# Queries turned unsplit two sequences ahead and stacked from DRAM, on a gated cross-attention block

## The reference

```python
q = relu(layernorm(x)); k = v = relu(ctx)            # per head of 32
att = softmax(q k^T / sqrt(32)); o = att v
x1 = x + tanh(g0) * relu(o @ ffn_w.T + ffn_b)
n = layernorm(x1); n_prev = n shifted by one token
xr = mu_r*n + (1-mu_r)*n_prev; xk likewise with mu_k
out = x1 + tanh(g1) * sigmoid(xr W_r) * (relu(xk W_k)^2 W_v)
```

## Time and profile before

| what | value |
|---|---|
| median of 3 runs | 2935.4 us (2933.75 to 2940.07) |
| the profiled execution | 2935.97 us |
| its span | 2934.1 us |
| mean granted clock of PE | 0.996 |
| busy share PEld, DVE, ACT, POOL | 74%, 80%, 53%, 36% |
| DMA | 408.56 MB, mean 139 GB/s |

### The profile page before, as it was taken

How to read it: one execution, slowest core, us unless ns; L and a number is a source line. 1 busy time by engine, 2 the same in 40 slices (tenths; PEclk the granted TensorE clock), 3 DMA queues, 4 the chain that set the end, 5 groups by cost and what they waited for, 6 DMA issues and landing times. The chain is left out here.

```text
span 2934.1 us, 71298 instructions
## 1 busy us (share of the span) xinstructions
PE 2833.1 (97%) x23168; PEld 2183.8 (74%) x23168; DVE 2349.9 (80%) x4175; ACT 1568.1 (53%) x2828; POOL 1044.8 (36%) x902
## 2 busy tenths in 40 slices
PE   3899999999999999999999999999999999999998
PEld 2677777777777777777777777777777777777776
DVE  5788888888888878878878878888888888888874
ACT  4455555555555555555555555555555555555552
POOL 0233333343343333333343333333333333333333
PEclk9999999999999999999999999999999999999999
DMA  5544545535445445445445445445445455355431
GB/s 167 153 129 145 154 121 151 155 121 154 151 123 156 143 127 159 138 130 159 138 131 159 133 138 155 129 145 153 126 147 156 121 152 154 122 154 149 126 104 42
DMA packets 405258, 408.56 MB, mean 139 GB/s; under 512 B 164577, under 2 KB 329441, under 8 KB 405218
## 3 DMA queue, kind: packets, MB, share of 16 engines
q1 hardware_dynamic: 352994, 340.92, 39.7%
q10 hardware_dynamic: 52224, 67.12, 7.0%
HBM read 272.64 MB, written 134.22 MB: 139 GB/s over the span
## 5 line engine op out<-in xcount | busy, mean ns | idle before, releaser
L699 DVE TENSOR_REDUCE m_nat<-bank 128x2 fp32r<-128x512 f32 x1024 | 694.6, 684 | 142.0 <-PE bank L906 141.5
L477 ACT ACTIVATE q_st<-bank 96x512 fp32r<-96x512 f32 x512 | 303.9, 593 | 765.7 <-PE bank L875 765.7
L496 ACT ACTIVATE probs<-bank 128x512 f32<-128x512 f32 x1024 | 593.6, 590 | 195.8 <-PE bank L918 187.2
L718 DVE RECIPROCAL o_val<-bank 128x256 f32<-128x256 f32 x256 | 449.3, 1755 | 60.4 <-PE bank L944 53.2
L918 PE MATMUL bank<-q_st,k_st 97*128 97x256 f32 x2048 | 437.9, 295 | 18.3 <-DMA q_st<-m_t 18.1
L906 PE MATMUL bank<-k_st,q_st 96*128 96x256 f32 x2048 | 430.0, 292 | 6.0 <-DMA k_st<-k_dram 4.5
L918 PEld LDWEIGHTS bank<-q_st,k_st 97*128 97x128 f32 x2048 | 345.5, 190 | 84.5 <-issue 22.6
L906 PEld LDWEIGHTS bank<-k_st,q_st 96*128 96x128 f32 x2048 | 356.8, 192 | 58.1 <-issue 5.9
L364 POOL TENSOR_TENSOR o_lo<-o_mv,o_hi 128x512 fp32r<-128x512 f32 x128 | 174.0, 1360 | 583.3 <-ACT o_hi L503 583.3
L397 POOL TENSOR_TENSOR xm<-xm 128x512 f32<-128x512 f32 x128 | 137.6, 1075 | 637.0 <-ACT xm L540 637.0
L708 DVE CAST m_t<-bank 4x256 fp32r<-4x256 f32 x256 | 105.1, 411 | 286.2 <-PE bank L884 286.1
(11 more groups left out here) (90 smaller groups left out, 5893.6 us busy)
## 6 DMA issues: line engine op xcount, KB each, us to landing
k_st<-k_dram SPq DMA_DIRECT2D x256, 256.0 KB, 3.6
k_raw<-ctx_t_dram SPq DMA_DIRECT2D x256, 128.0 KB, 3.1
x_ln<-x_dram SPq DMA_DIRECT2D x256, 128.0 KB
k_dram<-k_high SPq DMA_DIRECT2D x64, 512.0 KB, 3.0
k_dram<-k_raw SPq DMA_DIRECT2D x64, 512.0 KB, 4.5
k_st<-k_dram SPq DMA_DIRECT2D x256, 128.0 KB, 3.5
o_dram<-o_val SPq DMA_DIRECT2D x256, 128.0 KB, 1.7
o_mv<-o_dram SPq DMA_DIRECT2D x512, 64.0 KB, 2.0
```

What stands on the lines that cost most here:

```text
L477: nc.scalar.activation(q_st[0:QK, c, :, P * u:P * u + P], tp_bank[0:QK, :].rearrange("p (g t) -> p g t", g=GR), ACT.Copy).then_inc(q_stack ...
L496: nc.scalar.activation(probs[:, n // GR % 2, n % GR, :, :].rearrange("p v t -> p (v t)"), st_bank[n % 2][:, :], ACT.Exp, scale=SCALE).then ...
L699: nc.vector.tensor_reduce(m_nat[:, c % 2, :, n % GR:n % GR + 1], s_bank[n % 2][:, :].rearrange("p (u y) -> p u y", u=NU), AX_X, ALU.max, n ...
L718: nc.vector.reciprocal(o_val[:, :], pv_bank[:, T:2 * T]).then_inc(rden_ready, 1)
```

## The change

- `q_nat` now holds the normalised x of one sequence in float32, columns permuted (f, g) inside a group. `norm_1` writes it there, two sequences ahead. `turn_q` transposes each token half unsplit, four float32 products of 128 by 128; there are two turns a sequence.
- ACT's `q_copy` copies a turn with the ReLU into `q_raw`, `q_halve` makes `q_high`, DVE's `q_low` the rest, in place in `q_raw`. SP's `write_q` writes both to the new `q_dram`, 512 KB each. ACT's queue reads them back: `stack_q`, two DMAs for each of four groups (128 and 256 KB).
- `values(i-1, 3)` and `denominators(i-1, 3)` are in PE's step 0 instead of step 1, and DVE's `norm_o(i-1, 3)` stands before `copy_m(i, 1)`.
- `k_low(i+2)` on DVE moves from after `head_max(i+1, 6)` to after `copy_m(i+1, 0)`.
- SP does `write_k(i+2)` and then `write_q(i+2)` ahead of `read_o(i, 0)` and `write_o(i, 2)`.
- The first norm's statistics, `rstd_1`, `norm_1` and the load of x run one sequence earlier; the pipeline starts at i = -3.

```diff
+        q_dram = nc.dram_tensor("q_dram", [2, CH, 2, HD, GR, T], F32, kind="Internal").ap()
-        q_nat = sb("q_nat", [P, NU, HEADS, 3, HD], F32R)
+        q_nat = sb("q_nat", [P, NU, CH, P])
+        q_raw = sb("q_raw", [P, CH, T])
+        q_high = sb("q_high", [P, CH, T])
...
+            def write_q(b, par):
+                if on(b):
+                    sp.wait_ge(q_hi_ready, b + 1)
+                    sp.wait_ge(q_lo_ready, b + 1)
+                    for half, tile in enumerate((q_high, q_raw)):
+                        sp.dma_start(q_dram[par, :, half].rearrange("c f g t -> (f g) c t"),
+                                     tile[:, :, :]).then_inc(q_written, 16)
...
-                load_x(i + 2)
+                load_x(i + 3)
                 move_m(i, 3)
                 write_o(i, 1)
                 stack_k(i + 1, 2, 1 - par)
                 move_m(i + 1, 0)
                 load_w(i)
+                write_k(i + 2, par)
+                write_q(i + 2, par)
                 read_o(i, 0)
                 write_o(i, 2)
-                write_k(i + 2, par)
...
+            def stack_q(b, c, par):
+                if on(b):
+                    act.wait_ge(q_written, 32 * (b + 1))
+                    act.dma_start(q_st[0:HD, c, :, :].bitcast(F32), q_dram[par, c, 0]).then_inc(q_stacked[c], 16)
+                    act.dma_start(q_st[HD:QK, c, :, :].bitcast(F32),
+                                  q_dram[par, c].rearrange("h f g t -> (h f) g t")).then_inc(q_stacked[c], 16)
+            def q_copy(b, u):
+                if on(b):
+                    act.wait_ge(q_turned, NU * b + u + 1)
+                    after(act, q_written, 32 * b)
+                    nc.scalar.activation(q_raw[:, :, P * u:P * u + P],
+                                         tp_bank[:, :].rearrange("p (c t) -> p c t", c=CH),
+                                         ACT.Relu).then_inc(q_copied, 1)
+            def q_halve(b):
+                if on(b):
+                    act.wait_ge(q_copied, NU * (b + 1))
+                    nc.scalar.activation(q_high[:, :, :].bitcast(F32R), q_raw[:, :, :], ACT.Copy).then_inc(q_hi_ready, 1)
...
             def iteration(i, par):
                 weights_split(i)
-                q_stack(i, 2, 1)
+                stack_q(i, 3, par)
                 exponent(i, 0)
...
                 head_max(i, 7)
                 finish(i - 3, 1, 1 - par)
+                norm_o(i - 1, 3)
                 copy_m(i, 1)
-                norm_o(i - 1, 3)
                 mix_r(i - 2)
                 head_max(i, 8)
-                norm_1(i + 1)
+                norm_1(i + 2)
...
                 head_max(i + 1, 1)
+                q_low(i + 2)
                 head_max(i + 1, 2)
                 mix_k(i - 1)
                 head_max(i + 1, 3)
                 copy_m(i + 1, 0)
+                k_low(i + 2)
                 head_max(i + 1, 4)
-                stats_1(i + 2)
+                stats_1(i + 3)
                 finish(i - 2, 0, par)
                 head_max(i + 1, 5)
                 norm_o(i, 2)
                 head_max(i + 1, 6)
-                k_low(i + 2)
...
-                turns = [("q", i, 2, 1), ("m", i, 1, 0), ("q", i, 3, 0), ("q", i, 3, 1),
-                         ("m", i, 2, 0), ("q", i + 1, 0, 0), ("q", i + 1, 0, 1), ("q", i + 1, 1, 0),
-                         ("x", i - 1, 0, 0), ("m", i, 3, 0), ("x", i - 1, 0, 1), ("q", i + 1, 1, 1),
-                         ("m", i + 1, 0, 0), ("q", i + 1, 2, 0)]
+                turns = [("m", i, 1), ("q", i + 2, 0), ("m", i, 2), ("q", i + 2, 1),
+                         ("x", i - 1, 0), ("m", i, 3), ("x", i - 1, 1), ("m", i + 1, 0)]
...
                 shifted_scores(i, 0)
                 dense(0, 0)
+                values(i - 1, 3)
                 scores(i, 7)
+                denominators(i - 1, 3)
                 dense(0, 1)
                 shifted_scores(i, 1)
-                values(i - 1, 3)
-                turn(1)
-                denominators(i - 1, 3)
+                turn(0)
                 dense(0, 2)
                 scores(i, 8)
                 dense(0, 3)
-                turn(2)
```

More of the change, by code:

```diff
@@ L139, in flamingo_block @@
         q_turned = sem("q_turned")
-        q_stacked = sem("q_stacked")
+        q_copied = sem("q_copied")
+        q_written = sem("q_written")
+        q_stacked = [sem(f"q_stacked{c}") for c in range(CH)]
         v_ready = sem("v_ready")
@@ L207, in pipeline @@
         def pipeline(eng, iteration):
-            for i in range(-2, 4):
+            for i in range(-3, 4):
                 iteration(i, i % 2)
-            with eng.Fori(6, NB // 2 + 3) as pair:
+            with eng.Fori(6, NB // 2 + 2) as pair:
                 iteration(pair * 2 - 8, 0)
                 iteration(pair * 2 - 7, 1)
-            for i in range(NB - 2, NB + 3):
+            for i in range(NB - 4, NB + 3):
                 iteration(i, i % 2)
@@ L236, in load_x @@
                 if on(b):
-                    after(sp, q_lo_ready, 2 * b)
-                    after(sp, q_hi_ready, 2 * b)
+                    after(sp, x_normed, NU * b)
                     for m in range(GR):
@@ L591, in iteration @@
                 z_relu(i - 1, 0)
[L592 removed]
+                q_copy(i + 2, 1)
                 exponent(i, 7)
+                stack_q(i + 1, 1, 1 - par)
                 split_high(i, 6)
[L596 removed]
+                q_halve(i + 2)
                 exponent(i, 8)
@@ L666, in norm_1, with q_low @@
                     dve.wait_ge(rstd_ready, b + 1)
+                    after(dve, q_turned, NU * b)
                     for u in range(NU):
-                        nc.vector.tensor_scalar(x_ln[:, u, :], x_ln[:, u, :], mv[:, 0, u, 0:1], rstd[:, 0, u:u + 1],
+                        nc.vector.tensor_scalar(q_nat[:, u, :, :].rearrange("p c (f g) -> p c g f", g=GR),
+                                                x_ln[:, u, :].rearrange("p (c g f) -> p c g f", c=CH, g=GR),
+                                                mv[:, 0, u, 0:1], rstd[:, 0, u:u + 1],
                                                 ALU.subtract, ALU.mult).then_inc(x_normed, 1)
-            def q_low(b, u):
+            def q_low(b):
                 if on(b):
[L673 to L677, removed]
+                    dve.wait_ge(q_hi_ready, b + 1)
+                    nc.vector.tensor_tensor(q_raw[:, :, :].bitcast(F32R), q_raw[:, :, :], q_high[:, :, :],
+                                            ALU.subtract).then_inc(q_lo_ready, 1)
             def k_low(b):
@@ L1072, in iteration @@
                 shifted_scores(i, 3)
-                turn(3)
                 dense(1, 2)
@@ L1081, in iteration @@
                 dense(2, 1)
+                turn(1)
                 shifted_scores(i, 5)
@@ L1087, in iteration @@
                 values(i, 0)
-                turn(4)
+                turn(2)
                 denominators(i, 0)
                 shifted_scores(i, 6)
-                turn(5)
+                turn(3)
                 dense(3, 0)
@@ L1099, in iteration @@
                 scores(i, 14)
-                turn(6)
                 dense(3, 3)
@@ L1105, in iteration @@
                 scores(i, 15)
-                turn(7)
                 dense(4, 1)
@@ L1111, in iteration @@
                 values(i, 1)
-                turn(8)
+                turn(4)
                 scores(i + 1, 0)
                 dense(4, 3)
-                turn(9)
+                turn(5)
                 shifted_scores(i, 10)
@@ L1119, in iteration @@
                 denominators(i, 1)
-                turn(10)
+                turn(6)
                 scores(i + 1, 1)
@@ L1127, in iteration @@
                 dense(5, 3)
-                turn(11)
                 shifted_scores(i, 12)
@@ L1137, in iteration @@
                 values(i, 2)
-                turn(12)
+                turn(7)
                 scores(i + 1, 4)
@@ L1145, in iteration @@
                 denominators(i, 2)
-                turn(13)
                 dense(7, 1)
```

58 lines of the change are left out of this document (19 added, 39 removed).

## The result

The changed kernel takes 3171.98 us (median of 4 runs, 3169.44 to 3176.14) against 2934.57 us for the kernel before in the same comparison: a ratio of 1.0807, 95% interval 1.0788 to 1.0825. The forecast was 3050 us with a range to 3095. The direction was right, and the size was far off.

A forecast was written before the change was run, and what follows sets the result against it. The prediction took PE's instruction stream as the bound. Its terms, -1.45 + 1.41 + 2.3 - 0.53 = +1.73 us a sequence, 64 times 111, plus 3 for the start, made 2936 into 3050 us, range 2905 to 3095.

The forecast's parts named there:

- Step 1: PE's stream: eight query turns go, two float32 turns come, one change of product kind; net -1.45 us a sequence.
- Step 2: Values of group 3 on PE wait for their bank, DVE's product coming after the moved key halving: +1.41 us a sequence.
- Step 3: SP's read of groups 0 and 1 stands behind two megabytes of writes; PE waits 2.3 us at head 10.
- Step 4: What is hidden: PE's old wait for POOL is absorbed, -0.53 us a sequence; longer start costs 3 us once (0 to 6).
- the sum: -1.45 + 1.41 + 2.3 - 0.53 = +1.73 us a sequence, 64 times 111, plus 3: 3050 us.
- rival (d): PE's waits lower its clock each turn; 3 us at half clock cost 1.5, giving 3146 us and more; chance 0.07.
- a turn under 44.2 us: Sign that the forecast is wrong: one turn of the loop takes less than 44.2 us.
- an early read: Sign that the forecast is wrong: the read of groups 0 and 1 lands before 1415 on the turn's clock.
- PE's busy time was to fall by 93 us: Sign that the forecast is right: PE's busy time down by about 93 us while the span grows.
- Rival (a): The read of groups 0 and 1 isn't held up by the writes: 2913 us, or 2947 with POOL's wait; chance 0.22.
- Rival (b): Not slower, PE's stream decides because DVE's group 2 product comes early enough: 2846 us (2812 without POOL's wait); chance 0.12.

The follow-up runs named there:

- run 5: Changed kernel with q_low ahead of copy_m(i, 3), k_low ahead of copy_m(i + 1, 0), and each write on SP spread to match; 2915.3 us, ratio 0.9934.
- run 10: run 5 with the weights issued in the body of i = -2 and q_low behind norm_2(i - 1, 1); 2987.4 us, ratio 1.0179.
- run 2: Changed kernel with k_low back behind the maximum of head 6 and the key write back at the end of SP's body; 3033.0 us, ratio 1.0332.
- run 12: run 5 with key halving and key write where the change put them, only the query write spread; 2988.6 us, ratio 1.0183.
- run 1: Changed kernel with the read of groups 0 and 1 and the write of group 2 ahead of the key and query writes on SP; 3237.8 us, ratio 1.1018.
- run 4: Changed kernel with the edits of run 1 and run 2 together, both writes at the end of SP's body; 3250.3 us, ratio 1.1067.
- run 6: run 4 with each query write cut from 512 to 128 KB, group 0 alone, all groups stacked from it; 3018.4 us, ratio 1.0290.
- run 7: Changed kernel with 12 products that add zero, 1.4 us of PE work, ahead of head 10's scores; 3110.7 us, ratio 1.0600.

## Why the prediction was wrong in size and right in kind

**Step 1 (PE's stream)** was mis-sized: -1.45 us a sequence as worked out, -1.03 by PE's busy time in run 5. The two float32 turns were even a little cheaper than their row (0.36 us to the next start, not 0.42), so the error is in what goes: removing a turn gives back less than the distance it had in the timeline. Which products take it I didn't separate, and busy time isn't a pure count of the work: run 10, with the same products and the clock at 1.00 in the loop, is only 36 us under the earlier trace rows (2797.3).

**Step 2 (values)** held. Predicted 1.41, measured 1.32; taken away by run 2, shown alone by run 12 at 1.37.

**Step 3 (the read behind 2 MB)** held. Predicted wait at head 10: 2.3; measured 1.98 in the timeline above, 1.8 on average, and another 0.5 at head 2, which I had put inside it. DVE's reciprocal waits 2.32 us for POOL where 2.15 was predicted. The two waits for the read, 2.3 us in sum, are what I had for one. The pair of rows that the step rested on was read too simply: the read issued at 1422.32 waits in the program for the landing of the write issued at 1419.17, so the 3.15 us are that write's own way to its landing behind larger transfers, and not an order in the queue. That what SP issues behind the writes comes late is shown by runs 1, 4 and 6 instead.

**Step 4 (hidden)** held in the loop: PE no longer waits for POOL. The longer start was predicted at 3 us with a bound of 6 and is 35, which is 32 us of the miss. I followed the first scores only, and not the first moves of maxima: PE waits 14.4 us for one of them, 10.7 before. But PE's waits for moves grew by 10 us only (18.1 to 28.4 in all, nearly all of it in the start), so the rest of the longer start isn't explained.

**The step that failed** is the sum: it has no term for the clock. The fall of the clock was put at nothing there and left to rival (d), with a chance of 0.07, as an alternative to the sum, though it is a consequence of the sum's own waits: whoever forecasts 3.7 us of waits in 13 us must say what they do to the clock. It measured +1.4 us a turn (the mean of 0.97), some 90 of the 122 us between 3050 and 3172. The price in (d) was right: "3 us of it at half clock cost 1.5"; run 7 takes the fall away and gets back 1.1 a turn. The argument against (d), that the waits are split by long full stretches, is refuted: 1.3, 0.2 to 0.6 and 1.8 us with some 5 us of full work between them were followed by a fall in 44 of 50 turns, one wait of up to 2.3 us (run 6) in 17, and 1.4 with 0.5 (run 12) in none. The 3146 us of (d) were the nearest number in the text to the measured 3172, partly by luck: they have PE's stream 27 us too short and the start 32 us too short, and count every one of 64 turns in full.

In a balance a sequence: -1.03 stream, +1.3 values, +2.3 read, -0.5 POOL, +1.4 clock, together +3.5, against 3.4 measured in the middle turns. Over all 63 it is 3.25 (205 us), as the last turns, which run partly empty, lose less; 205 and 35 make the 240 us by which the span grew. The forecast had +1.73 and 3.

**What would have shown it wrong** was a turn under 44.2 us or an early read, and neither came. One of the signs of being right did fail: PE's busy time was to fall by 93 us and grew by 22. Rival (a) falls with the read, which ACT used 10.3 us after the first write. Rival (b), PE's stream deciding, is what run 5 gets close to, by other places for the same work.

The Trainium skill, page "DMA: Bandwidth & Descriptors", section "Queues, rings and completion order", has each DMA engine start the descriptors of a ring in order. Runs 1, 4 and 6 agree: what is late is always what SP issued behind the writes, and 0.8 MB less ahead of it is 2.1 us. What ACT's queue moves in the same stretch was not varied, so how the two queues share the DMA engines is not shown.

## What to carry to other kernels

A bulk write has two prices: its bytes, and the short transfers behind it in the queue. Before moving one, list every small DMA that follows it on that queue with its deadline, and put the write where the DMA engines and the computing engine are waiting anyway; here the same bytes, written at other places in the order, differ by 257 us. If a forecast contains waits of the bounding engine, add the clock that they cost, not as a rival but as a term of the sum. And undo one place at a time: the wait behind the one removed may be worse (runs 1 and 4).

## What the runs showed of the hardware that was not expected

Issuing a DMA takes longer right behind large writes in the same queue: the four reads behind four writes took 4.36 us of SP's time in the changed kernel and 1.83 before; the fourth write of 512 KB took 1.36 us, against 0.51 for the second of the same size. Full DMA engines alone don't do it: the stack of keys 3, issued a little later in the same turn, took 0.49 and 0.58 us with the engines just as full (the last row is a stretch as in the earlier trace rows; the DMA share stands next to last):

```profile
1546.55 0.49 SPq L272 DMA_DIRECT2D k_st<-k_dram  x1
1547.09 0.58 SPq L274 DMA_DIRECT2D k_st<-k_dram  x1
...
1547.00:1548.00 1.00, 1.00 (x9) 0.98 (x10) 0.96 (x2) 0.00 (x0) 0.00 (x0) 1.00 1.30 332
```

The same two took 0.83 and 1.38 us in run 4, right behind the writes. What follows on SP, and PE if it waits for that, is late by this time too. The clock fell without one long wait of PE: the longest in the turn shown was 1.98 us. Filling PE's idle time with products that add zero kept its granted clock at 1.00 and made the kernel 61 us faster.
